# A deeper tile ring, a changed item order and choices made early, in a four-layer transformer kernel

## The reference, cut to what matters

```python
x = x + attn_a(layernorm(x))      # 16 heads of 16, causal, output product with Wo
x = x + ffn(layernorm(x))
x = x + attn_b(layernorm(x))      # one head, inner residual and layernorm with gamma, beta
x = x + ffn(layernorm(x))

def ffn(x):
    t = x * rsqrt(mean(x * x) + EPS) * norm_scale
    logits = t @ gate_w + gate_b                # 8 experts
    top_v, top_i = top_k(logits, 2)             # the two best of each row
    w = softmax(top_v)
    y = sum over the two experts e: w_e * (swiglu(t @ w1[e] + b1[e]) @ w2[e] + b2[e])
    return x + y
```

## Time and profile before

| | us |
|---|---|
| median of three timed executions | 1760.12 |
| lowest and highest of the three | 1759.5, 1762.02 |
| the profiled execution, its own time | 1772.88 |
| its span | 1771.1 |

### The profile page before, as it was taken

The page is one execution under the profiler, slowest core; times in us unless marked ns, Lnnn a source line. Parts: engine busy times, 40 slices in busy tenths (PEclk is TensorE's granted clock), DMA queues, the critical chain, the costliest instruction groups (busy, mean ns, idle before and its releaser), DMA issues. The chain is left out here.

```text
span 1771.1 us, 35927 instructions
## 1 busy us (share of the span) xinstructions
PE 1643.6 (93%) x11154; PEld 1205.8 (68%) x11155; DVE 1278.3 (72%) x2671; ACT 1048.5 (59%) x1853; POOL 796.2 (45%) x779
## 2 busy tenths in 40 slices
PE   9889999999998894999999998799965999999998
PEld 4444444444442673999999997344534999999997
DVE  5688888888881666777777776368886777777776
ACT  4437767677676443666666664556654666666664
POOL 4541111111112122666666665225542666666664
PEclk9999999999998875999999999899975999999999
DMA  5654445254431752332222222301112222223232
GB/s 164 181 149 116 115 107 133 87 137 114 109 97 43 170 185 84 67 47 48 47 47 47 48 47 36 110 0 48 48 48 85 42 48 47 47 47 48 47 47 39
DMA packets 102684, 140.85 MB, mean 80 GB/s; under 512 B 18177, under 2 KB 86785, under 8 KB 99521
## 3 DMA queue, kind: packets, MB, share of 16 engines
q1 hardware_dynamic: 65382, 90.62, 19.5%
q0 software_dynamic: 31808, 37.32, 13.2%
q10 hardware_dynamic: 5402, 11.80, 1.9%
HBM read 74.21 MB, written 56.69 MB: 74 GB/s over the span
## 5 line engine op out<-in xcount | busy, mean ns | idle before, releaser
L596 ACT ACTIVATE a_Pt<-a_p_st 128x512 f32<-128x512 f32 (+2 forms) x624 | 302.5, 594 | 134.3 <-PE a_p_st L677 133.9
L623 DVE TENSOR_REDUCE mx<-a_p_sn 128x2 f32<-128x256 f32 (+1 forms) x600 | 333.7, 629 | 62.8 <-PE a_p_sn L660 52.7
L1362 ACT COPY R<-values_then_w 128x1024 f32 x284 | 283.0, 1044 | 38.9 <-issue 21.5
L1311 PE MATMUL e_p_g<-e_tT,R 128*128 128x128 f32 x2272 | 280.6, 277 | 1.6 <-ACT e_tT L1354 1.6
L1311 PE MATMUL e_p_l<-e_tT,R 128*128 128x128 f32 x2272 | 278.3, 276 | 0.0
L1323 PE MATMUL e_p_y<-w,e_hid 128*128 x1136 | 268.9, 380 | 5.8 <-DVE e_hid L1431 5.8
L1311 PEld LDWEIGHTS e_p_g<-e_tT,R 128*128 128x128 f32 x2272 | 268.3, 194 | 2.5 <-ACT e_tT L1354 2.4
L1311 PEld LDWEIGHTS e_p_l<-e_tT,R 128*128 128x128 f32 x2272 | 266.9, 193 | 0.1
L573 POOL TENSOR_SCALAR_AFFINE_SELECT a_Pt<-a_Pt 128x512 f32<-128x512 f32 x128 | 81.2, 635 | 366.1 <-ACT a_Pt L596 366.1
L1323 PEld LDWEIGHTS e_p_y<-w,e_hid 128*128 128x128 f32 x1136 | 205.0, 190 | 28.1 <-issue 6.2
L660 PE MATMUL a_p_sn<-Kst,Qst 96*128 96x128 bf16 (+1 forms) x720 | 220.9, 333 | 1.9 <-PEq L161 1.8
(11 more groups left out here) (224 smaller groups left out, 2396.2 us busy)
## 6 DMA issues: line engine op xcount, KB each, us to landing
qk_parts<-a_part SPq DMA_DIRECT2D x64, 192.0 KB, 3.1
a_Vst<-values_then_w SPq DMA_DIRECT2D x16, 512.0 KB, 18.3
o_rows<-a_OT ACTq DMA_DIRECT2D x32, 256.0 KB, 2.7
values_then_w<-in_mlp SPq DMA_DIRECT2D x16, 512.0 KB, 4.2
t_rows<-R SPq DMA_DIRECT2D x16, 512.0 KB, 3.0
Kst<-qk_parts SPq DMA_DIRECT2D x14, 384.0 KB
Qst<-qk_parts SPq DMA_DIRECT2D x14, 384.0 KB
a_Ot<-o_rows SPq DMA_DIRECT2D x64, 64.0 KB
```

The lines of the kernel that those rows point to most:

```text
L596: act.activation(weights(kb, slice(h, h + n), a, b), p_st[:, i % RING, 0:n * (b - a)].rearrange("p (n w) -> p n w", n=n), ACT.Exp, scale=D ...
L623: dve.tensor_reduce(mx[:, hs[0]:hs[-1] + 1, place], p_sn[:, (s + k) % RING, 0:w * len(hs)].rearrange("p (h w) -> p h w", w=w), AX.X, ALU.m ...
L1311: mm = pe.matmul(bank[:, s, c * P:(c + 1) * P], copied[:, s, k, at:at + P], tT[:, s, k * P:(k + 1) * P], start=(k == 0), stop=(k == KD - 1))
L1362: act.copy(copied[:, s, :, cols], g["w1"][:, bass.ds(e, 1), :, cols].rearrange("p a k n -> p (a k) n")).then_inc(copied_done, 1)
```

## The change

Four edits are made.

1. *Seam of `attend_a` and `out_rows`.* The second half of the output is copied to the tensor `xs`, which now exists from the start. ACT no longer waits for the last store of that half; SP does, in `out_rows`, ahead of the first load that reads what it wrote (load 12 of 16). Of the five DMAs of load 0, SP issues three and ACT two.
2. *Ring.* t in `out_rows` has a ring of 24 tiles, `R[8:32]`, six groups with a semaphore each. Only tiles 24 to 31 wait for a store, that of tile j-24's group.
3. *Items by tile halves.* In `layer_b`, `half, k = i // 2, i % 2`: items 0 and 1 are now the two feature halves of the first four tiles, items 2 and 3 those of the last four.
4. *Choices.* `layer_b` picks the experts of batches 0, 1 and 2 itself; the `rank` behind it picks only those of the last eight tiles (`picked = 24`), in instructions of 64 columns. The first `rank` stays as it is (`picked = 0`).

```diff
@@ attend_a
-    OT = mem.sb("OT", [P, 2, 512])
+    OT = [mem.sb("OT", [P, 512])[:, :], g["xs"][:, :, :].rearrange("p s d -> p (s d)")]
-    o_out = [mem.sem(f"o_out{c}") for c in range(2)]
+    o_out = [mem.sem("o_out0"), g["last_out"]]
...
-            for c in range(2):
-                act.wait_ge(o_out[c], 16 * U)
+            act.wait_ge(o_out[0], 16 * U)
@@ out_rows
+    T_GROUPS = 6
+    t_out = [mem.sem(f"t_out{s}") for s in range(T_GROUPS)]
-        return g["R"][:, 8 + j % 8, :]
+        return g["R"][:, 8 + j % (T_GROUPS * GROUP), :]
...
+                if q == NT // 2 - QB // 2:
+                    sp.wait_ge(g["last_out"], 16 * U)
...
-            load(0)
+            load_values(sp, 0, (0, 1, 2))
...
+            load_sums(act, 0)
+            load_values(act, 0, (3,))
...
-                if j >= 8:
-                    dve.wait_ge(tp_done, j - 7)
-                    dve.wait_ge(t_out[j // GROUP % 2], 16 * (j // 8))
+                if j >= T_GROUPS * GROUP:
+                    dve.wait_ge(tp_done, j - T_GROUPS * GROUP + 1)
+                    dve.wait_ge(t_out[j // GROUP % T_GROUPS], 16)
@@ rank
+def add_gate_bias(dve, link, g, L, at):
+    n = at.stop - at.start
+    link(dve.tensor_tensor(L[:, :, :], g["p_l"][:, at.start * E:at.stop * E]..., gb broadcast, ALU.add))
+def pick(dve, link, g, L, work, r, at):
+    link(dve.tensor_reduce(top, L[:, :, :], AX.X, ALU.max))
+    link(dve.tensor_tensor(work[:, :, :], L[:, :, :], top..., ALU.is_ge))
+    link(dve.tensor_tensor(work[:, :, :], work[:, :, :], rev, ALU.mult))
+    link(dve.tensor_reduce(place, work[:, :, :], AX.X, ALU.max))
+    link(dve.tensor_tensor(g["oh"][:, r, at, :], rev, place..., ALU.is_equal))
+def mask_first(dve, link, g, L, at):
+    link(dve.scalar_tensor_tensor(out=L[:, :, :], in0=g["oh"][:, 0, at, :], scalar=NEG, in1=L[:, :, :], ...))
+            at = slice(picked, NT)
@@ layer_b, turned and turn
-                k, half = i // 2, i % 2
+                half, k = i // 2, i % 2
@@ layer_b, DVE
+            def read_logits(b):
+                dve.wait_ge(l_done, QB // 2 * (b + 1))
+                add_gate_bias(dve, lambda ins: ins.then_inc(l_read, 1), g, L, slice(QB * b, QB * (b + 1)))
+            def first_picks(b):      # waits l_read, pick(0)
+            def second_picks(b):     # mask_first, pick(1)
...
+                        if b >= 2 and q == 5:
+                            read_logits(b - 2)
+                            first_picks(b - 2)
+                        if b >= 2 and q == 6:
+                            second_picks(b - 2)
                         for i in SCALED[early].get(q, ()):
                             scaled(back + i)
...
             scaled(back + 1)
+            read_logits(B - 2)
             residual_statistics(back + 6)
...
             for i in range(4, QB):
                 scaled(back + i)
+            first_picks(B - 2)
+            second_picks(B - 2)
@@ layer_b, PE
             for i in range(0, QB, 2):
                 turn_rows(back + i)
+                if i == 2:
+                    pe.wait_ge(l_read, B - 1)
```

More of the change, by code:

```diff
@@ L771, in out_rows @@
         mem.sem(s) for s in ("n_d", "t_d", "added", "tp_d", "tT_d", "l_d", "x_out"))
-    t_out = [mem.sem(f"t_out{s}") for s in range(2)]
+    T_GROUPS = 6
+    t_out = [mem.sem(f"t_out{s}") for s in range(T_GROUPS)]
     STEPS = NT + 10
@@ L823, in _ @@
             sp.dma_start(acc[T:T + P, :], g["X"][:, 0, :]).then_inc(x_out, 16)
-            for s in range(2):
-                sp.wait_ge(t_out[s], 16 * (NT // 8))
+            for s in range(T_GROUPS):
+                sp.wait_ge(t_out[s], 16 * len(range(s, NT // GROUP, T_GROUPS)))
             sp.wait_ge(x_out, 16 * (NT // GROUP + 1))
@@ L1459, in layer_b @@
     table = mem.sb("table", [P, 1])
+    L = mem.sb("L", [P, QB, E])
+    work = mem.sb("work", [P, QB, E])
+    chain, l_read = mem.sem("chain"), mem.sem("l_read")
     wn, wfT = square_weights(g)
@@ L1814, in residual_statistics, with link @@
                 statistics(2, j, x_of(j), st_done[2])
+            links = [0]
+            def link(ins):
+                links[0] += 1
+                ins.then_inc(chain, 1)
+                dve.wait_ge(chain, links[0])
+            def read_logits(b):
+                dve.wait_ge(l_done, QB // 2 * (b + 1))
+                add_gate_bias(dve, lambda ins: ins.then_inc(l_read, 1), g, L, slice(QB * b, QB * (b + 1)))
+            def first_picks(b):
+                at = slice(QB * b, QB * (b + 1))
+                dve.wait_ge(l_read, b + 1)
+                pick(dve, link, g, L, work, 0, at)
+            def second_picks(b):
+                at = slice(QB * b, QB * (b + 1))
+                mask_first(dve, link, g, L, at)
+                pick(dve, link, g, L, work, 1, at)
             def scaled(j):
@@ L2118, in program @@
         g["w1"] = g["VW"][:, :, :].rearrange("p (e k) n -> p e k n", k=KD)
+        g["xs"] = keep.sb("xs", [P, 2, D])
+        g["last_out"] = keep.sem("last_out")
         g["w_in"] = keep.sem("w_in")
@@ L2151, in program @@
         with ExitStack() as span:
-            g["p_l"] = Mem(nc, span).ps("p_logits1", [P, 512])
+            both = Mem(nc, span)
+            g["p_l"] = both.ps("p_logits1", [P, 512])
+            g["oh"] = both.sb("oh1", [P, 2, NT, E])
+            g["best"] = both.sb("best1", [P, 4, NT])
             phase(out_rows, "a3_", o_dram, t_dram, x_dram)
-            phase(rank, "r1_", t_dram, w_dram)
+            phase(rank, "r1_", t_dram, w_dram, 0)
         phase(experts, "e1_", t_dram, w_dram, x_dram, spent, True)
@@ L2158, in program @@
         with ExitStack() as span:
-            g["p_l"] = Mem(nc, span).ps("p_logits2", [P, 512])
+            both = Mem(nc, span)
+            g["p_l"] = both.ps("p_logits2", [P, 512])
+            g["oh"] = both.sb("oh2", [P, 2, NT, E])
+            g["best"] = both.sb("best2", [P, 4, NT])
             phase(layer_b, "b_", x_dram, t_dram, out)
-            phase(rank, "r2_", t_dram, w_dram)
+            phase(rank, "r2_", t_dram, w_dram, NT - QB)
         phase(experts, "e2_", t_dram, w_dram, out, [], False)
```

58 lines of the change are left out of this document (31 added, 27 removed).

## The result

The new kernel takes 1751.86 us (median of 8 executions, 1747.73 to 1754.58); beside it the kernel before took 1758.57 (8 executions, 1755.75 to 1762.02). The ratio is 0.9959, with a 95% interval of 0.9946 to 0.9973: 7.2 us less, between 4.7 and 9.5 (the medians themselves differ by 6.7). The forecast was 2.5 us less.

A forecast was written before the change was run, and what follows sets the result against it. PE, busy 93% of the span, bounds the kernel; gains lie where it waits or runs at half clock. Seam -2.4, waits -1.05, items -2.3, `rank` -2.4, logits +0.3, choices +5.4: -2.5 from 1760.12 gives 1757.6 us, range 1743 to 1762.

The forecast's parts named there:

- the forecast's own case: Whole kernel: no half clock in the timed executions and none new, 1757.6 us, range 1754.5 to 1760.5; chance 50%.
- the first rival: `out_rows`: the half clock is in the timed executions too, so the ring brings its 11.9 us there, 1745.7 us; chance 30%.
- the seam: Between `attend_a` and `out_rows`: SP starts 1.65 us earlier and load 0 is split over two queues; 2.4 us less.
- the ring: `out_rows`: DVE's two short waits for stores of t go, 1.05 us less; nothing counted for the third in timed executions.
- the items: `layer_b`: item 1 no longer waits for ACT; second batch 1.4, third 0.9, last nothing; 2.3 us less, bounds 1 and 3.
- the reading of the 12.8 us: Profiled 1772.88 against timed median 1760.12: the gap put down to `out_rows`' third wait and half clock, 11.9 us, profile only.
- the third rival: Third batch of `layer_b`: PE idle 2.4 us, its clock falls; 1762.7 us at least, 1769 at most; chance 12%.
- The 0.8 us for the split: Load 0 of `out_rows`: two of five issues, 0.44 us each, leave SP's queue for ACT's, about 0.8 us less.
- The choices: Third and last batch of `layer_b`: two groups of six small DVE instructions each, 5.4 us more, between 4.0 and 7.2.
- the upper end worked out for full exclusion: Step 6 of `layer_b`'s third batch: four choices each wait out a POOL instruction, so the group takes 3.6 us.
- The second list: Second `rank`: twelve links of 64 columns at 0.25 to 0.26 us instead of 0.457; 2.4 us less.
- The ring only moves the wait: `out_rows`: loads of `o_rows` come last, PE's `rows` waits and the clock falls there; 1759 us; chance 8%.

The follow-up runs named there:

- e12: The kernel before, unchanged, run against itself: 1758.4 us against 1759.28, ratio 0.9991.
- e10: The new kernel with a ring of 16 tiles for t in `out_rows` instead of 24: 1748.68 us, ratio 0.9925 to the kernel before.
- e1: The kernel before with only the ring of 24 tiles for t in `out_rows`: 1751.15 us against 1758.52, ratio 0.9949.
- e2: The kernel before with only the items by tile halves in `layer_b`: 1752.6 us, ratio 0.9964.
- e8: The new kernel with all five DMAs of load 0 issued by SP again: 1749.31 us, ratio 0.995 to the kernel before.
- e4: The kernel before with only the choices of batches 0 to 2 moved into `layer_b`: 1764.67 us, ratio 1.0016.
- e11: The new kernel with the items of `layer_b` numbered by feature half again: 1755.72 us, ratio 0.9967 to the kernel before.
- e7: The new kernel with the second group of six choices behind step 6's scaled rows, third and last batch: 1751.37 us, ratio 0.9962 to the kernel before.
- e6: The new kernel without the choices in `layer_b`, second list as before: 1745.28 us, ratio 0.9925 to the kernel before.
- e5: The new kernel with all choices of batches 0 to 2 in one group behind DVE's last scaled row of `layer_b`: 1743.53 us against 1757.31, ratio 0.9912.
- e9: The new kernel with the ring of 8 tiles for t in `out_rows` again: 1753.0 us, ratio 0.9963 to the kernel before.

## Why the prediction was right, and where it was not

The direction and the range held, the range by luck in part: 1751.86 us lies below what the forecast's own case allowed (1754.5 to 1760.5) and above what the first rival did (1742 to 1749), and is inside 1743 to 1762 only because that range was drawn over both. The forecast of 2.5 us was 4.7 short of the measured 7.2, and two of its terms were too small, one too large.

Of the signs named, the seam (0.51 us), the ring, the items and the links came as said, and so did the delay of the scaled row (PE turns it 13.27 us behind the maximum of step 21 instead of 10.52, 2.75 later). `layer_b` did not get longer by 2 to 4 us, but shorter by 0.5, as the items gained more. The profile became 21.8 us shorter and the median 6.7, which fits neither the sign for nor the sign against the reading of the 12.8 us. (In the third rival 1267.9 - 1265.4 is 2.5, not 2.4; nothing hangs on it.)

**The ring, the step that failed.** The prediction took the profiled execution as one of its own kind and counted "1.05 us plus nothing" for the timed ones. The runs show that it is one draw from the same executions: among the timed ones of the kernel before the slowest on the three chips took 1772.99, 1773.73 and 1771.60 us. Against its repetition e12 the 12.8 us are 10.9 in `out_rows` and 5.6 ahead of the seam, less 3.7 in the later stages. Of six profiles without the deeper ring, three have the half clock (96.97, 92.94, 91.44 us) and three have not (86.79, 86.81, 86.05). The seven with the ring of 24, and e10, lie between 83.1 and 84.5, 83.8 in the mean. So the ring is worth 2.7 us where the clock does not fall and 8 to 13 where it does, 6.4 in the mean of the six. Both poles of the prediction, 1.05 in every execution and 11.9 in every execution, were wrong. The timed runs agree with a term of several us: 9.0 for the ring alone (e1), 4.3 or 6.7 for 16 tiles against 8. And executions of one kernel on a chip with the ring of 24 spread by 3.8 to 7.8 us, those with the ring of 8 by 11.5 to 20.8 on the three chips of the experiments (12 to 34 executions each; the first eight of before only by 6.3, and the ring of 16 by 9.1). The 1.05 itself was low because a long wait in the kernel before takes the place of two or three short ones: e2 has four, 3.05 us. Why a store of t lands late in one execution and not in the next was not found.

**The seam.** SP's start came 1.71 us earlier as worked out (1.65). The 0.8 us for the split did not come. In five profiles with the old seam PE's first transpose stands 6.05 to 6.22 us behind ACT's last issue, with the new one 4.75 in the mean: 1.4 us, not 2.4. Without the split (e8) it is 4.83, so the issues that ACT takes over are not what PE waits for. The prediction took 0.44 us for an issue from rows of the old seam; right behind the last store it took 0.47 to 0.66. One thing was not foreseen: the stretch at half clock at the start of the stage lasts 10.2 us in all nine profiles with the new seam and 13.7 in all five with the old one. The stage is not visibly shorter for it (83.73 us in e1, 83.1 to 84.5 in the others with the ring of 24).

**Items by tile halves: 2.3 forecast, 3.7 to 3.8 measured.** The second batch gave 1.5 (1.4). The third gave 1.5 instead of 0.9. The prediction worked from the kernel before's trace, where the clock fell ahead of item 0 and so hid part of ACT's delay; in e1, e4 and e11 it falls only behind item 1, item 0 takes 0.63 us and item 1 waits 1.34. Against the kernel before the place gave 2.0, but the other 0.5 is that execution's longer stretch at half clock, not the edit. The last gave 0.7 instead of nothing, since PE did wait there for ACT. In two of six profiles with the old order the clock fell in the second batch as well, for 1.7 us more in steps 2 to 3 and 1.0 in steps 10 to 11. That may be part of the difference between 3.8 us in the steps and 6.3 (e2) or 7.0 (e11 against e10) in the timed runs; e11 against the new kernel gives 1.4. The interval of each ratio reaches some 4 us to either side, so the timed runs do not set these apart, and how much the edit is worth in them stays open.

**The choices: right in size, the path named in part.** 5.4 forecast, 2.76 + 2.54 = 5.3 measured, in the new kernel and in e4. The first group cost 1.53 (1.55). The second took 2.72 for six, less 0.57 of idle time and 0.84 of the scaled rows. In the third batch the path was the one named: the scaled rows come later, PE waits 1.89 us for them, and the maximum of step 24 waits 0.80 us for the scores behind them. What the prediction left out is that DVE's own chain is nearly as long, only 0.80 us shorter. So e7, which freed PE, gained nothing. In the last batch it is DVE alone: from 1272.56 to 1291.7 it has no idle time in the new kernel, where in e6 it has 1.38 and 0.69 us. The net price of this edit, 5.3 - 2.4 = 2.9 us, is lost in the new kernel; e5 shows that it need not be paid. Reading the logits cost nothing instead of 0.3. The Trainium skill's rule ("SBUF — State Buffer", "Who interferes with whom") told rightly who is slowed, instructions with two SBUF inputs and not the reductions; the upper end worked out for full exclusion, 3.6 us for the group, was not reached.

**The second list: right.** 26.94 to 24.54, 2.40 of 2.4; links of 0.257.

**The sum again.** Without any fall of the clock: -1.4 - 2.7 - 3.8 + 5.3 - 2.4 = -5.0. With the mean of what the profiles show of falls, 3.7 for the ring and 0.9 for the items (two of six by 2.7): -9.6. The measured interval, -9.5 to -4.7, holds the first and ends at the second; how often the falls come is known from six profiles only. The 6.2 us by which the new kernel's profile is ahead at the seam are none of it: over all profiles this point lies between 565.3 and 576.0, and the kernel before again has it at 570.3. So the profile was 7.4 us below the 1758.5 forecast for it by that 6.2 and by 3.9 more in `layer_b`, less 2.7 at the seam and in `experts`.

**The rivals.** "Half clock in the timed executions" was half right: in some. "The ring only moves the wait" is out; PE's waits for `a_Ot` in the stage are 1.6 us in four pieces. "Slower by a new half clock in the third batch" did not happen in the new kernel, but it did in e9, behind the same idle time of 1.89 us: one of the six profiles with this order of DVE's instructions (after, e4, e8 to e11). e7 shows it at 3.01 us, for 3.9 us. In the last batch a stretch of 3.4 us at half clock is new in all six, behind 2.37 us of idle time; it costs nothing that can be seen, since DVE sets the pace there. The limit put on the idle time, about 2.3 us, is not one: behind 1.47 us the clock fell (e9), behind 1.89 once in six, behind 1.95 and 1.34 it fell twice and stayed four times.

## What to carry to other kernels

When the profiled execution lies far above the timed ones, take it as one draw of a wait that varies, ask how often it happens, and cost the edit for both cases; a deeper ring earns its place by cutting off the bad draws, and 16 tiles would have done here. Put small DVE work where DVE waits for the stage to end, in one wide group, not in the steps where DVE sets the pace or is close to it: the choices of batches 0 and 1 cost 5.3 us in the steps, and widened to take them in, the group behind the last row cost nothing. Before freeing one path, look how much shorter the next one is. Before splitting the issues of a load over two queues, look whether the issue or the landing is what the reader waits for.
